# Attention scores by one product: the head's matrix folded into the keys, and whole float32 key tiles for the values

## What is computed

```
c_q  = h @ W_DQ  + b_DQ                       # 32 features
c_kv = h @ W_DKV + b_DKV                      # 32 features
q = concat(c_q @ W_UQ + b_UQ, c_q @ W_QR + b_QR)   # 8 heads, 128 + 32
k = concat(c_kv @ W_UK + b_UK, h @ W_KR + b_KR)    # 128 per head + 32 shared
v = c_kv @ W_UV + b_UV
attn = softmax(q k^T / sqrt(160))             # 4 x 8 heads x 1024 x 1024
o = (attn @ v) @ W_O + b_O
```

## Time and profile before

| | |
|---|---|
| median of 3 runs | 1004.86 us (1003.99 to 1005.87) |
| the profiled execution's own time | 1002.61 us |
| its span in the profile | 1000.9 us |
| busy in the span | PE 881.8, DVE 713.9, ACT 588.0, POOL 655.7 us |
| mean granted TensorE clock | 0.943 of full speed |

### The profile page before, as it was taken

How to read it: one execution, slowest core, us unless ns; L and a number is a source line. 1 busy time by engine, 2 the same in 40 slices (tenths; PEclk the granted TensorE clock), 3 DMA queues, 4 the chain that set the end, 5 groups by cost and what they waited for, 6 DMA issues and landing times. The chain is left out here.

```text
span 1000.9 us, 21467 instructions
## 1 busy us (share of the span) xinstructions
PE 881.8 (88%) x8406; PEld 527.7 (53%) x8406; DVE 713.9 (71%) x1315; ACT 588.0 (59%) x1004; POOL 655.7 (66%) x437
## 2 busy tenths in 40 slices
PE   4893899999999999999999988962499999999995
PEld 1350244444444444444444547862266777677764
DVE  4768888888888888888898836872075666566643
ACT  3750577777777777777777663664265446544650
POOL 4200599999999999999999993698404524442452
PEclk9995799999999999999999998985599999999998
DMA  9910000000000000000000004259525434543110
GB/s 279 339 43 0 1 2 2 2 2 2 2 2 2 2 2 2 2 2 2 2 2 1 3 1 169 99 198 320 201 69 162 143 107 140 175 142 123 43 52 19
DMA packets 48166, 71.61 MB, mean 72 GB/s; under 512 B 7508, under 2 KB 40473, under 8 KB 47938
## 3 DMA queue, kind: packets, MB, share of 16 engines
q1 hardware_dynamic: 38114, 53.13, 16.1%
q0 software_dynamic: 7680, 16.87, 5.2%
q10 hardware_dynamic: 2272, 0.24, 0.2%
HBM read 46.76 MB, written 29.67 MB: 76 GB/s over the span
## 5 line engine op out<-in xcount | busy, mean ns | idle before, releaser
L834 POOL TENSOR_TENSOR prob_lo<-prob 128x1024 f16<-128x1024 f32 x208 | 437.3, 2130 | 95.0 <-ACT prob L799 94.9
L799 ACT ACTIVATE prob<-st_ps 128x512 f32<-128x512 f32 x512 | 301.4, 597 | 131.8 <-PE st_ps L723 129.5
L859 DVE TENSOR_REDUCE part_max<-x_ps 128x1 f32<-128x512 f32 x512 | 325.1, 678 | 66.7 <-PE x_ps L733 65.7
L722 PE MATMUL st_ps<-QA,KA 128*128 128x512 f16 x512 | 198.1, 387 | 0.5 <-ACT prob L799 0.5
L723 PE MATMUL st_ps<-QB,KB 65*128 65x512 f16 x512 | 196.4, 384 | 0.0
L771 PE MATMUL acc_ps<-VV,prob 128*128 128x65 f16 x2048 | 159.3, 194 | 3.9 <-POOL prob_lo L834 3.9
L771 PEld LDWEIGHTS acc_ps<-VV,prob 128*128 128x128 bf16 x2048 | 143.6, 98 | 33.4 <-POOL prob_lo L834 6.1
L771 PE MATMUL acc_ps<-VV,prob_lo 128*128 128x65 f16 x2048 | 158.7, 194 | 0.0
L771 PEld LDWEIGHTS acc_ps<-VV,prob_lo 128*128 128x128 f16 x2048 | 134.9, 98 | 29.9
L1340 POOL DMA_INDIRECT out<-yo,xb x48 | 47.7, 993 | 153.3 <-DVE yo L1447 151.1
L732 PE MATMUL x_ps<-KA,QA 64*128 64x512 f16 x256 | 102.2, 399 | 20.8 <-DVE part_max L859 20.7
(11 more groups left out here) (177 smaller groups left out, 1346.7 us busy)
## 6 DMA issues: line engine op xcount, KB each, us to landing
w1f<-in_L_ffn_w SPq DMA_DIRECT2D x8, 1024.0 KB, 6.1
w2f<-in_L_ffn_w SPq DMA_DIRECT2D x8, 1024.0 KB, 6.1
xbuf<-zeros SPq DMA_DIRECT2D x7, 910.0 KB, 16.7
xb<-xbuf SPq DMA_DIRECT2D x8, 780.0 KB, 5.4
x<-in_L_attn_h_t SPq DMA_DIRECT2D x8, 512.0 KB, 8.9
out<-x SPq DMA_DIRECT2D x4, 1024.0 KB, 5.9
tbuf<-x SPq DMA_DIRECT2D x4, 1024.0 KB, 9.7
tbuf<-gb_row SPq DMA_DIRECT2D x4, 1024.0 KB, 4.7
```

What stands on the lines that cost most here:

```text
L722: mm(st_ps[i % 2][:], KA[:, at], QA[:, n % QRING, half], start=True, stop=False)
L799: nc.scalar.activation(prob[:, k, f * HALF:(f + 1) * HALF], st_ps[i % 2][:], ACT.Exp).then_inc(exp_done, 1)
L834: nc.gpsimd.tensor_tensor(prob_lo[:, k, :], prob[:, k, :], prob_top[:, k, :], ALU.subtract).then_inc(sub_pool, 1)
L859: nc.vector.tensor_reduce(part_max[:, n % 2, item // 2, item % 2:item % 2 + 1], x_ps[i % 3][:], AX.X, ALU.max).then_inc(smax_done, 1)
```

## The change

- The head's matrix (98 x 64, folded with both maps in stage one as GH and a low part GL, now with the key's features as rows) is applied to the keys instead of the queries. Once per head, after slot 4's scores, TensorE makes 98 key features of 1024 keys (four products, L754 and L757) in a bank that it shares with the maxima; ScalarE copies them to KX (L805), VectorE puts the low part into 33 of the rows (L858).
- A half of the scores is one product, KX with the latents CQ (L725), whose row 98 holds the maxima. The maxima are two 98-row products with the same bank pair (L744) and one reduction of 1024 columns (L852), which writes them where the DMA reads them. The turn by TensorE and the copy by ScalarE are gone. CQ is kept twice, by one DMA at the start of the stage; queries are dealt to tiles by stride 8.
- VectorE subtracts no `prob_lo`. Tiles 1 and 6 of even heads and tile 3 of odd heads (`whole`) are multiplied as float32 with V32, a float32 copy of the values, 8 products of 33 columns (L769). GpSimd keeps 6 tiles of even and 7 of odd heads.

The core of the diff:

```diff
-                        nc.vector.tensor_scalar(G[:, :, 0:DC], g_ps, SCALE, None, ALU.mult).then_inc(prep, 1)
...
+                        i = n - FOLD
+                        heads = slice(4 * i, 4 * i + 4)
+                        nc.vector.tensor_scalar(G[:, heads, :], bank[:].rearrange("p (h c) -> p h c", h=4)[:, :, 0:QROWS],
+                                                SCALE, None, ALU.mult).then_inc(side_done, 1)
+                        v.wait_ge(side_done, n + 1)
+                        nc.vector.tensor_copy(GH[:, heads, :], G[:, heads, :]).then_inc(prep, 1)
+                        v.wait_ge(prep, i + 1)
+                        nc.vector.tensor_tensor(GL[:, heads, :], G[0:LR, heads, :], GH[0:LR, heads, :], ALU.subtract)
...
+                    nc.vector.tensor_tensor(V32[:, tiles, 0:DC], v_ps[:, :, LR:LR + DC], VV[:, tiles, DC:2 * DC],
+                                            ALU.add).then_inc(v_done, 1)
...
-                    elif n == GQS:
-                        for h in range(H):
-                            last = mm(bank[0:QROWS, h * DC:(h + 1) * DC], uqT[:, h, 0:QROWS], ukvT[:, h, 0:DC], start=True, stop=True)
+                    elif n >= FOLD:
+                        for i in range(4):
+                            h = 4 * (n - FOLD) + i
+                            at = slice(i * P, i * P + QROWS)
+                            for r in (0, LR):
+                                mm(bank[r:r + DC, at], ukvT[:, h, 0:DC], uqT[:, h, 0:QROWS], start=True, stop=True)
+                                last = mm(bank[r + DC:r + LR, at], qr[:, h, :], ident[0:QROWS, 0:QROWS], start=True, stop=True)
...
-        QUERY_SLOTS = (4, 6)
+        KEY_SLOT = 4
+        def whole(n):
+            return (3,) if n % 2 else (1, 6)
+        def place_of_maxima(n, j):
+            return (9 * n + j + (j > KEY_SLOT)) % 2
+        def place_of_keys(n):
+            return (9 * (n - 1) + KEY_SLOT + 1) % 2
...
+                sp.dma_start(CQ[0:QROWS, 1, :], CQ[0:QROWS, 0, :]).then_inc(copied, 16)
...
-                    mm(st_ps[i % 2][:], KA[:, at], QA[:, n % QRING, half], start=True, stop=False)
-                    mm(st_ps[i % 2][:], KB[:, at], QB[:, n % QRING, half], start=False, stop=True).then_inc(scores_ready, 1)
+                    mm(st_ps[i % 2][:], KX[:, n % KRING, k * P:(k + 1) * P],
+                       CQ[:, n % 2, b * S + f * HALF:b * S + (f + 1) * HALF], start=True, stop=True).then_inc(scores_ready, 1)
...
+                    if j == KEY_SLOT + 1:
+                        te.wait_ge(smax_done, ST * n + j)
+                    elif j == KEY_SLOT + 2:
+                        if is_head(n + 1):
+                            te.wait_ge(kl_done, n + 2)
+                    elif ST * n + j >= 2:
+                        te.wait_ge(smax_done, ST * n + j - 1)
+                    bank = x_ps[place_of_maxima(n, j)]
+                    for f in HALVES:
+                        half = slice(f * HALF, (f + 1) * HALF)
+                        last = mm(bank[:, half], queries_of[:, n % 2, b * P:(b + 1) * P, j], KX[0:QROWS, n % KRING, half],
+                                  start=True, stop=True)
...
+                    if k in whole(n):
+                        te.wait_ge(exp_done, (n * ST + k) * 2 + 2)
+                        for q in range(ST):
+                            last = mm(acc_ps[:, q, DC:VC], prob[:, k, q * P:(q + 1) * P], V32[:, b * ST + k, :],
+                                      start=False, stop=False)
...
-                    if k in QUERY_SLOTS and is_head(p + 3):
-                        query(p + 3, QUERY_SLOTS.index(k))
+                    if k == KEY_SLOT and is_head(p + 3):
+                        keys(p + 3)
...
-                ac.wait_ge(q_ready, 2 * n + f + 1)
-                nc.scalar.activation(QA[:, n % QRING, f * HALF:(f + 1) * HALF], side_ps[:], ACT.Copy).then_inc(qa_done, 1)
+                ac.wait_ge(k_ready, n + 1)
+                nc.scalar.activation(KX[0:QROWS, n % KRING, :], x_ps[place_of_keys(n)][0:QROWS, :], ACT.Copy).then_inc(kh_done, 1)
...
-                nc.vector.tensor_tensor(prob_lo[:, k, :], prob[:, k, :], prob_top[:, k, :],
-                                        ALU.subtract).then_inc(sub_vector, 1)
+                at = KX[LR:QROWS - 1, n % KRING, :]
+                nc.vector.tensor_tensor(at, x_ps[place_of_keys(n)][LR:QROWS - 1, :], at, ALU.subtract).then_inc(kl_done, 1)
...
+                if is_head(p + 2):
+                    maxima(p + 2, k)
+                if k == KEY_SLOT + 1 and is_head(p + 3):
+                    keys_low(p + 3)
```

More of the change, by code:

```diff
@@ L142, in adaln_block @@
         ukvT = sb(one, "ukvT", [P, H, 2 * DC])
-        G = sb(one, "G", [QROWS, H, P])
+        G = sb(one, "G", [P, H, QROWS])
         zeros = sb(one, "zeros", [P, 7, ROW])
@@ L344, in _ @@
                 pool.wait_ge(ln_rstd, 2)
-                fill(13, CQ[3 * DC:QROWS, :], 1.0)
+                fill(13, CQ[3 * DC:QROWS, 0, :], 1.0)
                 pool.wait_ge(const_p, 14)
-                for g in range(2, NG):
+                power(2)
+                pool.wait_ge(ln_rstd, 3)
+                fill(14, V32[:, :, DC:DC + 1], 1.0)
+                pool.wait_ge(const_p, 15)
+                for g in range(3, NG):
                     power(g)
@@ L615, in _ @@
                 latent(2, 1)
-                side(GQS)
+                side(FOLD)
                 turn(7)
+                side(FOLD + 1)
                 values(2)
@@ L632, in adaln_block @@
         prob_lo = sb(two, "prob_lo", [P, ST, S], fp16)
-        part_max = sb(two, "part_max", [P, 2, ST, 2])
         raw = sb(two, "raw", [P, ST, VC - DC])
@@ L637, in adaln_block @@
         st_ps = [ps(two, f"st_ps{n}", [P, HALF]) for n in range(2)]
-        x_ps = [ps(two, f"x_ps{n}", [P, HALF]) for n in range(3)]
-        side_ps = ps(two, "side_ps", [P, HALF])
+        x_ps = [ps(two, f"x_ps{n}", [P, S]) for n in range(2)]
         acc_ps = ps(two, "acc_ps", [P, ST, P])
@@ L663, in adaln_block @@
         AHEAD = 4
-        QUERY_SLOTS = (4, 6)
-        FIRST_MAX = 0
-        ROW_SLOT = 1
-        def by_vector(n):
-            return (5, 7) if n % 2 else (5,)
+        KEY_SLOT = 4
+        queries_of = CQ[0:QROWS, :, :].rearrange("c r (g t) -> c r g t", t=ST)
+        def whole(n):
+            return (3,) if n % 2 else (1, 6)
         def by_pool(n):
-            return [k for k in range(ST) if k not in by_vector(n)]
+            return [k for k in range(ST) if k not in whole(n)]
         pool_before = [sum(len(by_pool(m)) for m in range(n)) for n in range(HEADS)]
-        vector_before = [sum(len(by_vector(m)) for m in range(n)) for n in range(HEADS)]
         def slots():
@@ new lines, in keys @@
+                def keys(n):
+                    b, h = n // H, n % H
+                    if n:
+                        te.wait_ge(smax_done, ST * (n - 1) + KEY_SLOT)
+                    bank = x_ps[place_of_keys(n)]
+                    for f in HALVES:
+                        mm(bank[0:QROWS, f * HALF:(f + 1) * HALF], GH[:, h, :],
+                           KA[:, b * S + f * HALF:b * S + (f + 1) * HALF], start=True, stop=False)
+                    for f in HALVES:
+                        last = mm(bank[0:QROWS, f * HALF:(f + 1) * HALF], GL[:, h, :],
+                                  KB[:, b * S + f * HALF:b * S + (f + 1) * HALF], start=False, stop=True)
+                    last.then_inc(k_ready, 1)
@@ L784, in _ @@
                             values(p, k)
[L785 to L788 removed]
+                        if f == 0 and is_head(p + 2):
+                            maxima(p + 2, k)
+                    if k == KEY_SLOT and is_head(p + 3):
+                        keys(p + 3)
                     if k < ST - 1 and is_head(p):
@@ L822, in _ @@
                             exponential(n, kk, f)
-                        if f == 0 and k == ROW_SLOT and is_head(p + 1):
-                            max_rows(p + 1)
                         if f == 0 and k == ST - 1 and is_head(p):
                             out_of_psum(p)
-                    if k in QUERY_SLOTS and is_head(p + 3):
-                        query(p + 3, QUERY_SLOTS.index(k))
+                    if k == KEY_SLOT and is_head(p + 3):
+                        keys(p + 3)
             @block.gpsimd
```

172 lines of the change are left out of this document (51 added, 121 removed).

## The result

| | before | after |
|---|---|---|
| median of the runs | 1004.42 us (4 runs) | 1067.03 us (4 runs, 1066.15 to 1068.54) |
| span of the profiled execution | 1000.9 us | 1064.1 us |
| mean granted TensorE clock | 0.943 | 0.893 |

The change makes the kernel slower: the ratio after to before is 1.063 (95% interval 1.06 to 1.066), 63 us. The forecast was 1008, with a range of 988 to 1028.

What follows compares the result with a forecast made beforehand. TensorE's in-order stream plus its waits for VectorE was taken as the bound, 15.40 us a head. Terms 5.8 - 2.6 - 2.1 + 2.2 = +3.3 us gave 1008 for the median, range 988 to 1028.

Steps and rivals of the forecast that it cites:

- the clock: TensorE's stream in the steady stretch was priced at a granted clock of 1.00.
- Rival E: Clock falls in even heads, where wait and whole tile lie together: 16 x 2.5 = 40 us more, 1048; chance 0.08.
- The new wait: TensorE stands before maxima(6) in every head until VectorE's keys_low ends: 1.8 us.
- The float32 tile: A whole tile on TensorE, 16 weight loads at 0.107 us each: 1.71 us.
- Rivals C: Float32 tiles on TensorE are cheaper, 1.33 us: 0.57 a head less, total 991; chance 0.12.
- D: Float32 tiles are dearer, 2.2 us or more, by unhidden columns or a drain: +0.7 a head, 1028; chance 0.15.
- GpSimd: Its subtractions all go in 1.85 us steps without VectorE's: 12.6 us a head, out of the ring, idling 3.
- The head: Steady head: stream 13.5, wait 1.8, key switches 0.2, boundary 0.15, together 15.6 us against 15.40.
- The lead-in: Attention's start up to its first score, keys made at half clock: +2.2 us, between 0 and 4.
- stage one: First stage, ended by VectorE, loses six operations of 3.9 us and gains others: 0, give or take 1.
- heads 29 to 31: Last heads: head 29 makes no keys, -2.6 us; heads 30 and 31 are GpSimd's, -2.1 us in the sum.
- Rival B: The key chain is covered and the 1.8 us wait vanishes: 13.8 a head, about 960; chance 0.12.

Runs made afterwards that it cites:

- e9_half_filled: Changed kernel with 12 small f16 products ahead of maxima(6) in each head, where TensorE otherwise stands still; 1033.57 us, ratio 1.029 to the kernel before.
- e6_low_none: Changed kernel with VectorE's keys_low ahead of the reduction of maxima(5) and no float32 tiles; 1002.71 us, ratio 0.997 to 1.001 to the kernel before.
- e2_low_first: Changed kernel with VectorE computing the keys' low part before the reduction of the maxima in slot 5; 970.8 us, ratio 0.966 to the kernel before.
- e5_low_one: e2_low_first with tile 3 alone as float32 in every head; 955.16 us, ratio 0.951 to the kernel before.
- e1_away: Changed kernel with the even heads' float32 tile moved from slot 6, behind the wait, to slot 3; 1045.73 us, ratio 1.041 to the kernel before.
- e4_no_whole: Changed kernel without float32 tiles, GpSimd subtracting all 8 tiles of a head, the wait kept; 1008.15 us, ratio 1.0035 to the kernel before.
- e7_filled: Changed kernel with 24 small f16 products ahead of maxima(6) in each head, where TensorE otherwise stands still; 1028.7 us, ratio 1.025 to the kernel before.
- e10_tile_behind: Changed kernel with the odd heads' float32 tile moved from 3 to 6, right behind the wait; 1091.12 us, ratio 1.085 to the kernel before.
- e8_every_other: Changed kernel with keys_low ahead of the reduction in odd heads only, the wait left in even heads; 1028.88 us, ratio 1.025 to the kernel before.

## Why the prediction was wrong

**The step that failed** is the clock: the sum takes the stream at a granted clock of 1.00, on the reason that "TensorE waits in every slot of the steady stretch and is granted 1.00; that is why E is small". Rival E named the place and the mechanism, and it is what happened, but it stood at 0.08, at 16 x 2.5 = 40, and outside the range. The waits of before were many and at most 0.9 long at the weight load (0.4 at the product); the new one is 2.0 and 1.66 in a piece, and the earlier trace rows had shown a fall behind standing. That row should have weighed more than the many short waits. The size failed too: a low stretch goes on for 6.8 us, not for the "2 to 3 us" of the tile and the products beside it, and there were 17 up to 590 us, in odd heads too: 51 us instead of 40. Without the clock the sum would have held: 1016, inside the range.

The Trainium skill (TensorE: Matmul & The Clock Gate, A second HAM failure mode) tells of a kernel whose clock swings because TensorE idles briefly between groups of products. I had held the trace against it. The runs here agree with it for single stands of 1.3 to 1.7 us (14 to 21 falls in 460 us), and in e9_half_filled for 0.94 us (7 falls); for the shorter waits of before and of e6_low_none, up to 0.98 us, they don't (no fall in the steady heads).

Point by point:
- **The new wait**, forecast 1.8: 1.66 on the engine, and 1.5 a head by the books, e2_low_first keeping 0.2 (4.5 us in 21 times on PE). Right.
- **The float32 tile**, 1.71 from three loads in 0.41 us: 1.71 in e2_low_first. Rivals C (1.33) and D (2.2 or more) fall, and with D the time of 2.2 that followed from the rule of the Trainium skill (TensorE: Matmul & The Clock Gate, Part 3), which the trace spoke against already. A tile's step from e2_low_first to e5_low_one, 14.45 - 13.84 = 0.61 for half a tile, is 1.71 - 0.48 halved.
- **GpSimd** in steps of 1.85 once VectorE's subtraction is gone: its 208 subtractions show a mean of 1893 ns and no row of 2.96. Right; it idles 211 us.
- **The head**, 15.6: 15.9 where no fall comes. The sum lacked 0.3, over 29 heads 9 us; where they lie was not tried, but they are not in the wait: e2_low_first takes 14.45, where the sum's other terms and the 0.2 left of the wait give 13.5 + 0.2 + 0.15 + 0.2 = 14.05.
- **The lead-in**, +2.2: from the attention's first product to its first score are 22.93 us against 20.12, +2.8, about right. But the first product starts 2.6 us sooner (83.35 against 85.99), where I had 0 give or take 1 for stage one. Together +0.2, so this miss and the head's 0.3 partly cancel:

```profile
83.35 1.06 PE L754 MATMUL x_ps<-KA,GH 128*98 128x512 f16 x2 [8.59 <-PEq L200]
...
106.28 0.63 PE L725 MATMUL st_ps<-CQ,KX 99*128 99x512 f16 x1
```

- **The sum without the clock**: 1008 forecast, 1016 by the books, inside the range. The terms of heads 29 to 31 were not tried apart.
- **Rival B**, the wait covered, 960: e2_low_first is that kernel, at 971. It didn't happen by itself, as TensorE comes to the maxima too early, just as argued.

**What stays open.** Why one stand of 1.66 us is followed by a fall and the next isn't (after: every even head, four odd ones; e1_away: two stands with different ends; e4_no_whole: its stands of 1.2 us in even heads are followed, those of 1.45 in odd heads not), why six falls remain in e7_filled, and why e6_low_none, with 0.98 us in each head, has none where e9_half_filled, with 0.94, has seven. What TensorE does in the stand and behind it changes the number of falls, as e7_filled, e9_half_filled and e10_tile_behind show; that is no rule that tells a single fall.

## What to carry to other kernels

Price a new wait on TensorE twice: its own length, and the low clock behind it, which here cost as much again (45 and 51 us) and hides in the busy share, since TensorE is busy while slow. Many short waits are not a witness for one long one. Before trading work between engines, look whether the wait can be reordered away: one swap of two calls on VectorE turned 6% slower into 3% faster, and then the balance between the two engines that were left (e5_low_one, 5% faster) could be read off their busy shares.

## What the runs showed of the hardware

- One stand of TensorE of 1.3 to 1.7 us can be followed by 3.4, 6.8 or even 10.2 us at a granted clock of 0.50, beginning as much as 2.9 us after it works again (e8_every_other: it works from 325.97, and the clock is 0.92 in the step from 328 to 329 and 0.50 in the next).
- The stretch is longer when float32 products run in it: 3.4 us in e4_no_whole, in e1_away and in the four odd heads of after; with a tile behind the wait 6.8, or 10.2 where it begins 0.6 to 1.1 us ahead of the tile (e10_tile_behind, five times; after, from 164). Where it begins with the tile over or nearly so, it is 3.4 again (e8_every_other from 328.8, e7_filled from 266.1, 0.5 us before the tile's end).
- TensorE busy 86% with its waits in pieces, the longest 0.98 us, keeps 1.00 (e6_low_none); busy 98% in the records is no guarantee (e7_filled, six falls).
- A float32 product of 33 columns is two records and costs 2 x 0.107 us at full clock (16 records in 1.71). That is the step of two weight loads of 128 columns in the kernel before (0.11), so the columns hide.
